# Scores of sixteen heads in a two-layer attention kernel: even and odd heads on the two halves of TensorE's rows

## The reference, cut to what matters

```
qh, kh, vh = proj(q, W_q, b_q), proj(k, W_k, b_k), proj(v, W_v, b_v)   # [B, 16 heads, rows, 8]
scores = einsum('bhqd,bhkd->bhqk', qh, kh) / sqrt(8)
scores = where(mask == 0, -1e9, scores)
attn = softmax(scores, axis=-1)
context = einsum('bhqk,bhkd->bhqd', attn, vh)
return context @ W_o.T + b_o
```

## Time and profile before

| | |
|---|---|
| median of the runs | 821.77 us |
| profiled execution | 817.71 us |
| its span | 815.8 us |
| TensorE matmul, busy | 700.3 us (86%), 7289 instructions |
| TensorE weight load, busy | 484.9 us (59%) |
| VectorE, busy | 564.3 us (69%), 1227 instructions |
| ScalarE, busy | 515.7 us (63%), 787 instructions |
| GpSimd, busy | 260.3 us (32%), 304 instructions |
| matmuls of L705 (scores) | 1536, in two groups of 768 |
| matmuls of L718 (weighing) | 3072 |
| matmuls of L632 (MX) | 336 |

### The profile page before, as it was taken

The page is one execution under the profiler, slowest core; times in us unless marked ns, Lnnn a source line. Parts: engine busy times, 40 slices in busy tenths (PEclk is TensorE's granted clock), DMA queues, the critical chain, the costliest instruction groups (busy, mean ns, idle before and its releaser), DMA issues.

```text
span 815.8 us, 19683 instructions
## 1 busy us (share of the span) xinstructions
PE 700.3 (86%) x7289; PEld 484.9 (59%) x7289; DVE 564.3 (69%) x1227; ACT 515.7 (63%) x787; POOL 260.3 (32%) x304
## 2 busy tenths in 40 slices
PE   3699999975568898899899999998999998699997
PEld 3577777763215566556655655665665565467776
DVE  5799999977766887877877878777767674511111
ACT  4577777763254776776776786777777767344431
POOL 3488888881251203213221230231232020000000
PEclk9899999997557999999999999999999999599999
DMA  3122222434526167247336535733754470111110
GB/s 132 38 76 92 98 75 75 141 96 45 114 56 143 29 142 160 55 108 159 85 78 155 114 84 120 159 73 89 161 104 100 83 175 2 45 38 32 53 39 23
DMA packets 59504, 74.39 MB, mean 91 GB/s; under 512 B 35336, under 2 KB 40194, under 8 KB 59450
## 3 DMA queue, kind: packets, MB, share of 16 engines
q1 hardware_dynamic: 59450, 73.65, 37.9%
HBM read 32.61 MB, written 1.40 MB: 42 GB/s over the span
## 4 chain that ended last, share of the span: by engine, by line
PE 56%; DVE 27%; issue 9%; ACT 5%; POOL 2%; DVEq 1%; ACTq 0%
DVE mx L1511 10%; PE ps L718 8%; PE ps L632 6%; PE ps L778 6%; PE ps L790 6%; PE ps L618 6%; PE ps L705 6%; PE ps L624 4%; PE ps L518 3%; DVE ss L1217 3%; DVE rden L1520 2%; PE ps L532 2%; PE ps L655 2%; ACT arena L855 2%; DVE arena L1237 2%
## 5 line engine op out<-in xcount | busy, mean ns | idle before, releaser
L1511 DVE TENSOR_REDUCE mx<-ps 128x1 f32<-128x500 f32 x336 | 216.8, 674 | 77.5 <-PE ps L632 75.2
L967 ACT ACTIVATE P<-ps,kbias,kscale 125x896 f32<-125x896 f32 x192 | 210.1, 1097 | 48.2 <-PE ps L705 44.2
L632 PE MATMUL ps<-KP,Qb 128*128 128x500 bf16 x336 | 131.9, 393 | 17.5 <-DVE mx L1511 14.3
L718 PE MATMUL ps<-P,Vp 125*32 125x112 f32 x3072 | 113.4, 265 | 2.0 <-ACT P L967 1.3
L1062 POOL TENSOR_TENSOR KP<-kvall,KP 128x1500 bf16<-128x1500 f32 x16 | 48.6, 3036 | 196.3 <-ACT KP L911 196.3
L518 PE MATMUL ps<-wkv,cT 128*125 128x256 f32 x384 | 92.0, 383 | 0.7 <-ACT arena L868 0.7
L718 PEld LDWEIGHTS ps<-P,Vp 125*32 125x32 f32 x3072 | 67.1, 109 | 40.3 <-issue 29.3
L518 PEld LDWEIGHTS ps<-wkv,cT 128*125 128x125 f32 x384 | 69.5, 190 | 9.8 <-issue 1.0
L705 PEld LDWEIGHTS ps<-QS,KS 128*128 128x128 bf16 x768 | 55.5, 99 | 32.2 <-issue 16.6
L705 PEld LDWEIGHTS ps<-QS,arena 128*128 128x128 bf16 x768 | 53.3, 98 | 32.7 <-issue 20.2
L705 PE MATMUL ps<-QS,KS 128*128 128x112 bf16 x768 | 69.8, 214 | 3.5 <-DVE QS L1517 2.5
(11 more groups left out here) (204 smaller groups left out, 1058.3 us busy)
## 6 DMA issues: line engine op xcount, KB each, us to landing
cT<-ctxT_dram SPq DMA_DIRECT2D x32, 750.0 KB, 4.4
KS<-KP SPq DMA_DIRECT2D x48, 375.0 KB, 7.2
arena<-KP SPq DMA_DIRECT2D x48, 375.0 KB, 7.3
QS<-QD SPq DMA_DIRECT2D x96, 28.0 KB, 5.7
wgu<-w_dram SPq DMA_DIRECT2D x8, 256.0 KB, 3.1
silu<-w_dram SPq DMA_DIRECT2D x8, 256.0 KB, 2.9
x<-xh_dram SPq DMA_DIRECT2D x1, 512.0 KB, 3.5
mixed<-att SPq DMA_DIRECT2D x16, 28.0 KB
```

The source lines that it names most:

```text
L632: ins = nc.tensor.matmul(ps[:, bank, 0:KCW], q[:, 128 * c:128 * c + 128], KP[par][0][:, KCW * k:KCW * k + KCW], start=True, stop=True)
L718: ins = nc.tensor.matmul(ps[r:r + PW, 7, c:c + PAIRW], Vp[par][0:TK, t, p, :], P[t % 2][0:TK, PAIRW * p:PAIRW * p + PAIRW], start=(t == 0 ...
L967: nc.scalar.activation(P[t % 2][0:TK, :].rearrange("p (k n) -> p k n", k=2), src, ACT.Exp, scale=kscale[0:TK, bass.ds(n, 1)], bias=kbias[0 ...
L1511: ins = v.tensor_reduce(mx[:, c, k:k + 1], ps[:, bank, 0:KCW], AX.X, ALU.max)
```

## The change: what it does

Each pair's scores are no longer one matmul of 128 rows and 112 columns but two of 64 rows and 56 columns: h = 0 takes rows 0 to 63 (even head), h = 1 rows 64 to 127 (odd head). The two write to different PSUM banks. So a bank now holds the 8 even or the 8 odd heads, and `P` is ordered by even and odd heads; the weighing reads the two heads of a pair 448 columns apart. The moving queries need no mask: `QS` shrinks to 448 columns, `QD` to 56 per pair, `pmask` and its load go. The maxima stand in rows 0 and 64. `Qb`'s head mask is permuted so that the maxima come in the new order. VectorE's copies at SH get a wait for the stacking DMAs of their window.

```diff
@@ -44,7 +44,6 @@
 STACK = len(KEY_PART)
 ROWS = 2 * DK
 STRIDE = 8
-ONES = 0
 TWO_ONES = 1.0 + 127 * 2.0 ** -16
 KSW = NPAIR * S2 + 128 - TK
 
@@ -184,7 +183,7 @@
 
 
 def build(nc, xh, ctxT, m0, m1, gates, rows, bq, bk, wkv0, wq0, dense0, wg0, wu0, wd0, wq1, wk1, wv1, wo1,
-          gatew, w1, b1, w2, b2, bv, ident_in, hmask_in, hmask1_in, pmask_in,
+          gatew, w1, b1, w2, b2, bv, ident_in, hmask_in, hmask1_in,
           den_sel_in, rank_in, out):
     with ExitStack() as ctx:
         def sb(name, shape, dt=F32):
@@ -215,7 +214,6 @@
         hmask = sb("hmask", [128, H])
 
         hmask1 = sb("hmask1", [128, H])
-        pmask = sb("pmask", [128, 2])
         bv_sb = sb("bv_sb", [128, 2])
         den_sel = sb("den_sel", [128, 128])
         rank = sb("rank", [128, NT, E])
@@ -292,12 +290,12 @@
         krest = kvall[:, :, :].rearrange("p b n -> p (b n)")[:, 0:S2]
 
         QP = [sb(f"QP{k}", [128, 2, 128], BF16) for k in range(3)]
-        QD = [[sb(f"QD{n}_{k}", [128, 2, S], BF16) for k in range(3)] for n in range(2)]
+        QD = [[sb(f"QD{n}_{k}", [128, S], BF16) for k in range(3)] for n in range(2)]
 
         KSF = [sb("KS0", [128, KSW // 2 + 1])[:], arena[:, 0:KSW // 2 + 1]]
         KS = [k.bitcast(BF16)[:, 0:KSW] for k in KSF]
         two_ones = sb("two_ones", [128, 1])
-        QS = [sb(f"QS{n}", [128, HQ], BF16)[:] for n in range(2)]
+        QS = [sb(f"QS{n}", [128, HQ2], BF16)[:] for n in range(2)]
 
         Qb = [sb(f"Qb{n}", [128, H, S], BF16) for n in range(2)]
         Vp = [sb(f"Vp{n}", [128, T, NPAIR, PW]) for n in range(2)]
@@ -375,7 +373,7 @@
                 pair0(i)
 
             for dst, src in ((dense_sb[:], dense0), (wgu[:, 0, :], wg0), (wgu[:, 1, :], wu0), (wdn[:], wd0),
-                             (mi[0:TK, :], m1), (hmask1[:], hmask1_in), (pmask[:], pmask_in),
+                             (mi[0:TK, :], m1), (hmask1[:], hmask1_in),
                              (bv_sb[:], bv), (bq_sb[:], bq), (bk_sb[:], bk), (wq1_sb[:], wq1), (wk1_sb[:], wk1),
                              (wv1_sb[:], wv1), (wo1_sb[:], wo1), (den_sel[:], den_sel_in), (rank[:], rank_in),
                              (gw_sb[:], gatew), (b2_sb[:], b2)):
@@ -431,7 +429,7 @@
                 sp.wait_ge(sem("q_ready"), b + 1)
                 for j, part in enumerate(QUERY_PART):
                     sp.dma_start(spread(QS[par], j).rearrange("r (p n) -> r p n", p=NPAIR),
-                                 QD[par][part][:].rearrange("p k s -> p (k s)")).then_inc(sem(f"stacked{par}"), 16)
+                                 QD[par][part][:]).then_inc(sem(f"stacked{par}"), 16)
 
             def pair1(i):
                 for par in range(2):
@@ -473,7 +471,7 @@
                          xd).then_inc(sem("out_done"), 16)
             sp.wait_ge(sem("out_done"), 16)
 
-        LATE = 18 * 16
+        LATE = 17 * 16
 
 
         @block.tensor
@@ -640,7 +638,7 @@
                         for k in range(2):
                             lo, hi = max(128 * c, HQ2 * k), min(128 * c + 128, HQ2 * k + HQ2)
                             if lo < hi:
-                                r = ONES + 32 * k
+                                r = HALF * k
                                 ins = nc.tensor.matmul(ps[r:r + 1, bank, lo - HQ2 * k:hi - HQ2 * k],
                                                        mneg[:, c:c + 1], identb[:, lo - 128 * c:hi - 128 * c],
                                                        start=True, stop=True)
@@ -702,9 +700,10 @@
                     pe.wait_ge(sem("p_ready"), n - 1)
                 for p in range(4 * k, 4 * k + 4):
                     c0 = S2 * p + TK * t
-                    ins = nc.tensor.matmul(ps[:, 2 * (t % 2) + k, PAIRW * (p % 4):PAIRW * (p % 4) + PAIRW],
-                                           KS[par][:, c0:c0 + 128], QS[par][:, PAIRW * p:PAIRW * p + PAIRW],
-                                           start=True, stop=True)
+                    for h in range(2):
+                        rows = slice(HALF * h, HALF * h + HALF)
+                        ins = nc.tensor.matmul(ps[:, 2 * (t % 2) + h, S * p:S * p + S], KS[par][rows, c0:c0 + 128],
+                                               QS[par][rows, S * p:S * p + S], start=True, stop=True)
                 if k == 1:
                     ins.then_inc(sem("sc_ready"), 1)
 
@@ -713,10 +712,10 @@
                 pe.wait_ge(sem("p_ready"), n + 1)
                 if t == 0 and not (first and par == 0):
                     pe.wait_ge(sem("o_ready"), b)
+                heads = P[t % 2][0:TK, :].rearrange("p (k q s) -> p q k s", k=2, q=NPAIR)
                 for p in range(NPAIR):
                     r, c = PW * (p % 4), PAIRW * (p // 4)
-                    ins = nc.tensor.matmul(ps[r:r + PW, 7, c:c + PAIRW], Vp[par][0:TK, t, p, :],
-                                           P[t % 2][0:TK, PAIRW * p:PAIRW * p + PAIRW],
+                    ins = nc.tensor.matmul(ps[r:r + PW, 7, c:c + PAIRW], Vp[par][0:TK, t, p, :], heads[:, p, :, :],
                                            start=(t == 0 and p < 4), stop=(t == T - 1), skip_group_check=True)
                 ins.then_inc(sem("pv_done"), 1)
 
@@ -1081,9 +1080,8 @@
                 nc.gpsimd.tensor_tensor(Qb[par][:], bc(QP[0][:, z, HALF * par:HALF * par + S], 1, [128, H, S]),
                                         bc(hmask1[:], 2, [128, H, S]), ALU.mult).then_inc(sem("qb_ready"), 1)
                 for k in range(3):
-                    ins = nc.gpsimd.tensor_tensor(QD[par][k][:], bc(QP[k][:, z, HALF * par:HALF * par + S], 1,
-                                                                    [128, 2, S]),
-                                                  bc(pmask[:], 2, [128, 2, S]), ALU.mult)
+                    ins = nc.gpsimd.tensor_tensor(QD[par][k][:], QP[k][:, z, HALF * par:HALF * par + S],
+                                                  onesf[:, 0:S], ALU.mult)
                 ins.then_inc(sem("q_ready"), 1)
 
             def deviation(n, j):
@@ -1512,10 +1510,11 @@
                 elif unit == "SH":
                     if not (fixed(b) and b < 2):
                         dve.wait_ge(sem("sc_ready"), T * (b - 1))
+
+                    dve.wait_ge(sem(f"stacked{par}"), loads(b, par, 2 * STACK))
                     for k in range(2):
-                        r = ONES + 32 * k
-                        ins = v.tensor_copy(QS[par][ONES:ONES + 1, HQ2 * k:HQ2 * k + HQ2],
-                                            ps[r:r + 1, bank, 0:HQ2])
+                        r = HALF * k
+                        ins = v.tensor_copy(QS[par][r:r + 1, :], ps[r:r + 1, bank, 0:HQ2])
                 elif unit == "DEN":
                     ins = v.reciprocal(rden[:], ps[:, bank, 0:2 * PAIRW])
                 else:
@@ -1701,6 +1700,7 @@
     bv = np.zeros((4, PW, 2), f)
     bv[:, 1:1 + 2 * DK] = v["L1_xattn_b_v"].reshape(2, 4, 2 * DK).transpose(1, 2, 0)
     order = np.arange(D).reshape(NPAIR, 2 * DK).T.reshape(D)
+    halves = np.arange(H).reshape(NPAIR, 2).T.reshape(H)
     b2 = np.zeros((ND, E, ND, D), f)
     for t in range(ND):
         b2[t, :, t] = v["L1_ffn_b2"]
@@ -1736,8 +1736,7 @@
         "b2": b2.reshape(ND * E, ND, D),
         "ident_in": np.eye(128, dtype=f),
         "hmask_in": np.repeat(np.eye(H, dtype=f), DK, axis=0),
-        "hmask1_in": np.repeat(np.eye(H, dtype=f), DK, axis=0)[order],
-        "pmask_in": np.repeat(np.eye(2, dtype=f), HALF, axis=0),
+        "hmask1_in": np.repeat(np.eye(H, dtype=f), DK, axis=0)[order][:, halves],
         "den_sel_in": sel,
         "rank_in": np.broadcast_to(np.arange(E, 0, -1).astype(f), (128, NT, E)),
     }
```

## The result

The changed kernel takes 849.77 us (median of 4 runs, 848.37 to 855.72) against 821.03 us for the kernel before: ratio 1.0379, 95% interval 1.0343 to 1.0415. That is 28.7 us slower by the medians, whose own ratio is 1.035, and 31 us by the ratio on record. The forecast was 838 in a range of 822 to 860, so sign and range held, and the size was 16.5 of 28.7. The missing 12 us are not a wrong price of what I had listed, but two things that I had not listed: a stall for the loop's code, and the clock behind it.

A forecast was written before the change was run, and what follows sets the result against it. TensorE's instruction order was taken as nearly full, but not alone (DVE 27% of the chain). 7.5 window pairs x +2.2 us = +16.5 on 817.7 gave 834.2, 838 for the median; own range 830 to 850, wider range 822 to 860.

The forecast's parts named there:

- The half step: Score matmuls on TensorE: 8 narrow ones side by side take 112 ns, saving 85 ns per half step.
- The loads: Weight loads of the score matmuls: starts some 15 ns apart, eight in a row 120 ns, the half step's other limit.
- The change of shape: Between 64-row and 128-row matmuls on TensorE: each change costs 95 ns in both directions, 87 added per window pair.
- Rival 1: Score matmuls and their neighbours: no cost between 64 and 128 rows, so faster, 807 us; chance 13%.
- the sum on the chain: Chain of waits in a window pair: 42 changes less 23 half-step savings, +2.0 us, the lower bound; +2.2 taken.
- The last window: Final attention window, no units between its halves: can only save, at most 2.0 us; taken as 0.
- The seam, POOL and DMA: Copies between windows with their new wait, smaller query products, DMAs and setup: all taken as 0.
- Sum: Whole kernel: 817.7 us profiled plus 16.5 gives 834.2; forecast for the median 838.
- rival 2: Score matmuls: the two row halves take turns, no saving, +30 to +43 us, 852 to 865 us; chance 13%.
- the clock: TensorE's granted clock, 1.00 in the steady windows: forecast wrong if it leaves 1.00; no size or chance given.

The follow-up runs named there:

- before_mx64: Kernel before with all MX products over rows 0 to 63 only, adding 62 changes of shape per pair of windows; 842.86 us, ratio 1.0261.
- fill_unrolled: Changed kernel with TensorE's windows written out instead of looped and 6 unread matmuls at each seam between windows; 833.51 us, ratio 1.0169.
- full_unrolled: Changed kernel with every score matmul over all 128 rows (results wrong) and TensorE's windows written out instead of looped; 820.61 us, ratio 1.0013.
- after_unrolled: Changed kernel with TensorE's attention windows written out one after another instead of a loop; 843.74 us, ratio 1.0277.
- full_rows: Changed kernel with every score matmul over all 128 rows, still 8 per half step (results wrong), loop kept; 839.03 us, ratio 1.0207.
- same_half: Changed kernel with TensorE's windows written out and both heads' scores on rows 0 to 63 (results wrong); 865.91 us, ratio 1.0554.
- mx_unrolled: Changed kernel with TensorE's windows written out and most MX products over the 64 rows where queries are not zero; median 843.01 us.

## Why the prediction was right, and why it was too small

**The half step** was to take 112 ns; it takes 117 (94 from the first start to the last in the undisturbed windows, and 23 of streaming). The saving is 80 ns instead of 85. The loads did not set the pace: two start 3 ns apart, like their matmuls, and a pair of matmuls follows the last after 26 ns, once 38.

**The change of shape** was to cost 95 ns. It is 93 out of the narrow shape (116 ns from the last score matmul to L630, less 23), and 106 into it from L630 (317 ns, less the 211 between L632 and the scores in the earlier trace rows), 96 from the f32 products of keys and values (515 ns instead of 419, and 205 instead of 109). The drain that the Trainium skill's page "TensorEngine Tiling (Array Packing)", section "Key Properties", has for a change of tiling mode holds for row halves too, as L803 had shown. Rival 1 is out: before_mx64 pays for nothing but these changes, 2.6 us per pair.

**How much of it counts.** The sum on the chain, +2.0 per pair, rounded up to 2.2, met a measured +2.1 (fill_unrolled), with the clock at 1.00, or +2.4 with a loop on both sides (60.56 against 58.18) and +2.3 with none on either. By the prediction the cost was to lie between 2.0 and 4.2; that nearly all of what is off the chain is hidden fits the measured size, but no run takes it apart. PE's waits for VectorE's banks fell from 2.5 us per pair to 1.3, not below 1. Over all windows the sum is as close. VectorE's timeline has the first seam copy and the one ahead of the last window, first in the kernel before, then in fill_unrolled:

```profile
250.79 1.24 DVE L1517 CAST QS<-ps 1x448 bf16<-1x448 f32 x2 [0.75 <-PE ps L644]
...
675.04 1.24 DVE L1517 CAST QS<-ps 1x448 bf16<-1x448 f32 x2 [0.57 <-PE ps L644]
```

```profile
249.30 1.25 DVE L1525 CAST QS<-ps 1x448 bf16<-1x448 f32 x2 [0.75 <-PE ps L645]
...
689.97 1.25 DVE L1525 CAST QS<-ps 1x448 bf16<-1x448 f32 x2 [0.75 <-PE ps L645]
```

That is 424.25 and 440.67 us, +16.4 where 16.5 were forecast. The last window, which is not in this and which I had left at 0, gives 0.9 back, and fill_unrolled's profile came to its first window 1.5 us sooner, as its clock rose sooner in the preparation. By the medians the shapes cost 12.9 us (833.5 - 820.6), or 13.3 against the kernel before of the same session.

**The seam, POOL and DMA** at nothing: right to what the medians can tell. full_unrolled has the new wait, the strided read and the smaller products, and stands at 1.0013. No wait of the copies is put down to a DMA.

**What was not in the sum.** What fell short is the step "Sum": it held the price of the shapes alone, and I had counted the instructions of a half step only for their time. Twice as many score matmuls and loads also make the loop's code longer, 1,939 records per pair instead of 1,557, and this body is fetched again on each round. At the three jumps back TensorE stands over 3 us. Behind each, the clock falls for 6.8 us, so that such a window is some 4.6 us longer (35.1 against 30.5): 14 us in the profile, enough for the missing 12. That 849.8 still lies in the range of 822 to 860, and at the very edge of the forecast's own 830 to 850, is luck: neither range was laid out for a stall or a fall of the clock, and the wider one reaches so far for rival 2, which did not happen.

The prices of the two don't add up one by one. Writing the loop out gives 18.4 us back with full shapes (839.0 to 820.6), but only 6.0 with narrow ones (849.8 to 843.7), since without the stall the clock falls at the seams anyway. Filling the seams then gives 10.2 more (843.7 to 833.5). So the 28.7 us, taken apart in this order, are 6 for the loop's code, 10 for the clock at the seams, 13 for the shapes, and no more than 1 for the rest. These medians come from different sessions; by the ratios, each to the kernel before of its own session, the parts are 8, 9, 13 and 1 of 31 us, so each is known to some 2 us. I had named the clock as what would make the forecast wrong, but gave it neither a price nor a chance, because the rows of the steady windows said 1.00. That is a level and does not say how near it is to falling.

Two things stay open. What exactly distinguishes a seam at which the clock falls from one at which it doesn't was not settled: full_unrolled and after_unrolled have nearly the same waits there, and the one keeps 1.00 and the other falls once per pair. The narrow matmuls or the drains around them may have a part in it, but they are neither needed, as full_rows fell once at such a seam, nor enough, as same_half kept 1.00 at most of them. And the size at which a loop's code stops staying in the engine was only bracketed.

The Trainium skill's page "Runtime: NRT & Kernel Launch", section "Instruction fetch mechanics", says that code comes in blocks of 16 KiB, 256 instructions, and that a jump to a page not held stalls the engine. The 16 KB packets of q8 and the stalls of 3 us agree. It gives TensorE room for 2,048 instructions; by that figure alone a body of 1,939 would have stayed, while in these traces it is fetched anew on each round. It also says that this store is a FIFO whose window for jumps is 2 pages; by that even the 1,557 of the kernel before would have been fetched, and they were not. The traces decide against both.

## What to carry to other kernels

Narrow matmuls pay only where they stand together: here a half step saved 80 ns, and the changes of shape around it cost 93 and 96 to 106. With neighbours of 64 rows too (mx_unrolled) steps 3 to 10 of the windows became shorter than before, with the clock at 1.00. Before doubling the instructions of a loop, count the loop's instructions on that engine and look at the instruction queue in the DMA view: where it carries nothing during the loop, as in the kernel before, no code is fetched, and that can be lost. A granted clock of 1.00 is worth a price of its own in the forecast as soon as a change adds gaps to the engine.

## What the runs showed of the hardware

- A change between 64-row and 128-row matmuls costs 93 ns out of the narrow shape and 96 to 106 into it, like one between column shapes (0.09 us).
- Two matmuls on the two row halves start 3 to 4 ns apart and stream together: 8 of 56 columns in 117 ns, and 217 when all are on one half (194 from first to last start, and 23). Loads of 64 rows and 128 columns last 95 ns on record like those of 128 rows (98).
- A loop with 1,557 records per round on TensorE fetched no code for 177 us (363.5 to 541); one with 1,939 fetched 25 packets of 16 KB in the same stretch and stood 3.0 to 3.5 us at the jump back.
- The clock fell to 1.2 GHz for 6.8 us behind stalls of 3.0 to 3.5 us in five of six cases (three in the changed kernel, two of three in full_rows), and for 3.4 us behind the sixth. At seams with waits of 0.5 to 0.9 us it fell for 3.4 us once per pair in after_unrolled, once in all in full_rows, and in full_unrolled and the kernel before not at all from 310 to 600 us. Six matmuls in the idle time of a seam, read by nobody, made the kernel 10 us faster (843.74 to 833.51).
